# A stream of attention maxima shifted by 75 of a group's 144 events, and unread products in TensorE's waits

## The reference

```python
h = _layernorm(x) * (1 + ca) + sa
q, k, v = split(h @ W_qkv.T + b_qkv)                  # 16 heads of 16, 2 x 2048 tokens
logits = einsum('bhqd,bhkd->bhqk', q, k) / sqrt(16);  causal mask
attn = softmax(logits);  o = einsum('bhqk,bhkd->bhqd', attn, v)
x = x + ga * (o @ W_out.T + b_out)
h = _layernorm(x) * (1 + cb) + sb
x = x + gb * mole(relu(mole(h, W1, ...)), W2, ...)    # base product + softmax-routed low-rank experts
```

## Time and profile before

| | |
|---|---|
| median of three runs | 1465.85 us (1465.51 to 1467.76) |
| profiled execution | span 1465.0 us from its first to its last instruction; the page gives no other time of it |
| TensorE busy | 1309.6 us, 89% |
| VectorE busy | 1022.1 us, 70% |
| ScalarE busy | 773.8 us, 53% |
| GpSimd busy | 172.6 us, 12% |
| mean granted TensorE clock | 0.921 of full |
| attention | 134 to 1119 us: first group's maxima alone from 142 to 232 us, eight groups from 232 to 1113 us |
| last stage | 1119 to 1465 us |

### The profile page before, as it was taken

How to read it: one execution, slowest core, us unless ns; L and a number is a source line. 1 busy time by engine, 2 the same in 40 slices (tenths; PEclk the granted TensorE clock), 3 DMA queues, 4 the chain that set the end, 5 groups by cost and what they waited for, 6 DMA issues and landing times. The chain is left out here.

```text
span 1465.0 us, 25799 instructions
## 1 busy us (share of the span) xinstructions
PE 1309.6 (89%) x8432; PEld 679.2 (46%) x8432; DVE 1022.1 (70%) x1862; ACT 773.8 (53%) x1009; POOL 172.6 (12%) x101
## 2 busy tenths in 40 slices
PE   4993899999999998999998999999994599999997
PEld 3872223333333333333433433433221588888886
DVE  4893997886886885886887688688300466666664
ACT  2771004665665664666565666566793244444443
POOL 1468100000000000000000000000001122222221
PEclk8996557999999999999999999999997699999999
DMA  6345400002102101200210300200003102222200
GB/s 204 123 165 165 131 1 11 21 16 58 33 18 50 40 17 35 56 19 15 65 26 4 74 18 16 63 6 5 10 8 91 44 1 58 58 57 57 57 14 29
DMA packets 75812, 71.07 MB, mean 49 GB/s; under 512 B 17816, under 2 KB 68704, under 8 KB 75688
## 3 DMA queue, kind: packets, MB, share of 16 engines
q1 hardware_dynamic: 75688, 69.51, 16.9%
HBM read 47.57 MB, written 21.23 MB: 47 GB/s over the span
## 5 line engine op out<-in xcount | busy, mean ns | idle before, releaser
L854 DVE TENSOR_REDUCE mx<-ps 128x1 f32<-128x512 f32 (+3 forms) x1120 | 692.2, 669 | 170.8 <-PE ps L726 105.8
L808 ACT ACTIVATE prob<-ps 128x1024 f32<-128x1024 f32 (+3 forms) x640 | 546.7, 895 | 413.8 <-PE ps L751 260.0
L723 PE MATMUL ps<-kst,qst 96*128 96x512 bf16 (+3 forms) x1280 | 426.4, 374 | 28.4 <-DMA kst<-qk_parts 24.3
L747 PE MATMUL ps<-qst,kst 99*128 99x512 bf16 (+3 forms) x1280 | 362.2, 355 | 11.2 <-issue 7.5
L763 PE MATMUL ps<-prob,vw 128*32 128x512 f32 (+3 forms) x2560 | 303.8, 547 | 0.2
L723 PEld LDWEIGHTS ps<-kst,qst 96*128 96x128 bf16 x1280 | 120.7, 99 | 334.7 <-DVE mx L854 244.9
L747 PEld LDWEIGHTS ps<-qst,kst 99*128 99x128 bf16 x1280 | 118.9, 99 | 147.5 <-ACT prob L808 51.1
L751 PE MATMUL ps<-mask_k,ident_bf 128*128 128x128 bf16 x512 | 106.2, 227 | 0.0
L726 PE MATMUL ps<-mask_q,ident_bf 128*128 128x128 bf16 x512 | 106.0, 232 | 0.0
L926 POOL COPY vw<-v_nat 128x1024 f32 (+1 forms) x8 | 8.3, 1044 | 766.3 <-PE ps L763 766.3
L763 PEld LDWEIGHTS ps<-prob,vw 128*32 128x32 f32 x2560 | 51.0, 109 | 102.0 <-issue 79.6
(11 more groups left out here) (144 smaller groups left out, 1429.5 us busy)
## 6 DMA issues: line engine op xcount, KB each, us to landing
qk_parts<-parts SPq DMA_DIRECT2D x32, 384.0 KB, 2.9
qst<-qk_parts SPq DMA_DIRECT2D x192, 64.0 KB, 2.6
kst<-qk_parts SPq DMA_DIRECT2D x192, 64.0 KB, 2.5
xs<-in_x SPq DMA_DIRECT2D x16, 512.0 KB, 6.3
o_rows<-o_sb SPq DMA_DIRECT2D x128, 32.0 KB, 1.7
o_raw<-o_rows SPq DMA_DIRECT2D x16, 256.0 KB
rd<-rden_rows SPq DMA_DIRECT2D x16, 256.0 KB
out<-y SPq DMA_DIRECT2D x8, 512.0 KB, 3.2
```

The source lines that it names most:

```text
L723: last = pe.matmul(at, q[0:QK_ROWS, J, h0 + h, i % 4 * P:(i % 4 + 1) * P], k[0:QK_ROWS, cb, h0 + h, 0:width], start=True, stop=not diagonal)
L747: last = pe.matmul(ps[:, h, 0:width], kst[c][0:ST_ROWS, t // 4, h, t % 4 * P:(t % 4 + 1) * P], qst[c][0:ST_ROWS, J, h, skip:BLK], start=Tr ...
L808: act.activation(prob[:, n % P_BUFS, 2 * pair:2 * pair + 2, 0:width], ps[:, 2 * pair:2 * pair + 2, 0:width], ACT.Exp).then_inc(exp_done, 1)
L854: dve.tensor_reduce(mx[:, h0:h0 + nh, i % 4, cb], ps[:, bank, 0:nh * width].rearrange("p (h x) -> p h x", h=nh), AX, ALU.max).then_inc(max ...
```

## The change

The stream of events is shifted. `AHEAD` = 69: a group's first 69 events ride in the group before it, in tiles 21 to 39, and its last 75 (the rest of block 2 and block 3, with their turns) in the group itself, in tiles 0 to 20. Block 2's turn (event 86) then comes at tile 4.7 and block 3's (event 143) at tile 20.7, ahead of the tiles 12 and 24 that need them; those of blocks 0 and 1 come at tiles 24.7 and 32.7 of the group before. Ahead of the first group 69 events are made alone instead of 144, and the last group carries 75 instead of none. Every tile has 3.6 events, from its first place on. In SyncE's order the rows of the maxima of blocks 2 and 3 are now written within the group, those of 0 and 1 late in the group before; k and the last q block of the group after next are loaded last; the reciprocals are stored after all of these. VectorE's program is the same but that `invert` comes at product 35.

Beside it TensorE makes products that nobody reads (`UNREAD`): 24 (bf16, 512 columns) after the last sums of attention, and 58, 40 and 12 (fp32r, 512 columns) ahead of `project_out(0)`, `turn(0)` and `route_in(0)`. They wait for nothing and release nothing.

```diff
@@ -90,22 +74,29 @@
 EV = max_events()
 NEV = len(EV)
 assert NEV % S_BUFS == 0
-FIRST_SLOT = 7
 SLOTS_OF_TILE = 3
 
 
+
+AHEAD = 69
+TURN_EVENT = [EV.index(("turn", J)) for J in range(NJ)]
+NEAR_UNITS = [J for J in range(NJ) if TURN_EVENT[J] < AHEAD]
+OWN_UNITS = [J for J in range(NJ) if TURN_EVENT[J] >= AHEAD]
+INVERT_AT = NMU // 4
+
+
 def event_slots():
 
-    slots, done = [], 0
-    for u in range(SLOTS_OF_TILE * NKT):
-        want = min(NEV, max(0, (u - FIRST_SLOT) * NEV // (SLOTS_OF_TILE * NKT - FIRST_SLOT - 2)))
-        slots.append(range(done, want))
-        done = want
-    slots[-1] = range(slots[-1].start, NEV)
-    return slots
+    count = SLOTS_OF_TILE * NKT
+    return [range(u * NEV // count, (u + 1) * NEV // count) for u in range(count)]
 
 
 SLOTS = event_slots()
+
+
+
+
+UNREAD = (24, 58, 40, 12)
 
 
 def alone(eng):
@@ -665,44 +656,59 @@
 
 
 
-            def sync_step(sp, s, c, hs, cur, nxt, far):
-                nhs = hs + c
-                nc_ = 1 - c
-                for J in range(NJ):
-                    if nxt:
-                        sp.wait_ge(max_red, (s + 1) * NEV + EV.index(("turn", J)) + 1)
-                        for a in range(NPART):
-                            sp.dma_start(qst[nc_][QK_ROWS + a:QK_ROWS + a + 1, J],
-                                         mT[a * 16:(a + 1) * 16, J, :]).then_inc(m_in[nc_][J], 16)
-                    if cur and far and J < NJ - 1:
-
+            def load_maxima(sp, s, c, J):
+
+                sp.wait_ge(max_red, s * NEV + TURN_EVENT[J] + 1)
+                for a in range(NPART):
+                    sp.dma_start(qst[c][QK_ROWS + a:QK_ROWS + a + 1, J],
+                                 mT[a * 16:(a + 1) * 16, J, :]).then_inc(m_in[c][J], 16)
+
+            def store_out(sp, s, c, hs, J):
+
+                sp.wait_ge(o_out, s * NJ + J + 1)
+                cols = slice(c * S + J * BLK, c * S + (J + 1) * BLK)
+                for h in range(GH):
+                    sp.dma_start(o_rows[bass.ds(hs * GH + h, 1), :, cols]
+                                 .rearrange("o r t -> (o r) t"),
+                                 o_sb[2 * HD * h:2 * HD * h + HD, J % 2, :]
+                                 ).then_inc(o_stored[J % 2], 16)
+
+                    sp.dma_start(den[32 * J + 8 * h:32 * J + 8 * h + 8, c, :],
+                                 o_sb[2 * HD * h + HD:2 * HD * h + HD + 1, J % 2, :]
+                                 ).then_inc(den_in[J % 2], 16)
+
+            def sync_step(sp, s, c, hs, nxt, far):
+
+                def queries(J):
+                    if far:
                         sp.wait_ge(st_done, s * 2 * NKT + 2 * (1 + max(n for n in range(NKT) if KT[n][0] == J)))
                         load_q(sp, c, hs + 1, J)
-                    if cur and far and J == NJ - 1:
-
-                        sp.wait_ge(st_done, (s + 1) * 2 * NKT)
-                        for j in range(NJ):
-                            load_k(sp, c, hs + 1, j)
-                        load_q(sp, c, hs + 1, J)
-                    if cur:
-                        sp.wait_ge(o_out, s * NJ + J + 1)
-                        cols = slice(c * S + J * BLK, c * S + (J + 1) * BLK)
-                        for h in range(GH):
-                            sp.dma_start(o_rows[bass.ds(hs * GH + h, 1), :, cols]
-                                         .rearrange("o r t -> (o r) t"),
-                                         o_sb[2 * HD * h:2 * HD * h + HD, J % 2, :]
-                                         ).then_inc(o_stored[J % 2], 16)
-
-                            sp.dma_start(den[32 * J + 8 * h:32 * J + 8 * h + 8, c, :],
-                                         o_sb[2 * HD * h + HD:2 * HD * h + HD + 1, J % 2, :]
-                                         ).then_inc(den_in[J % 2], 16)
-                    if cur and J == 1 and not (isinstance(s, int) and s == 0):
-                        store_rden(sp, s - 1, 1 - c, hs - 1 + c)
+
+                load_maxima(sp, s, c, OWN_UNITS[0])
+                for J in NEAR_UNITS:
+                    queries(J)
+                    store_out(sp, s, c, hs, J)
+                for J in OWN_UNITS[1:]:
+                    load_maxima(sp, s, c, J)
+                for J in OWN_UNITS[:-1]:
+                    queries(J)
+                    if nxt:
+                        load_maxima(sp, s + 1, 1 - c, NEAR_UNITS[0])
+                    store_out(sp, s, c, hs, J)
+                for J in NEAR_UNITS[1:]:
+                    if nxt:
+                        load_maxima(sp, s + 1, 1 - c, J)
+                if not (isinstance(s, int) and s == 0):
+                    store_rden(sp, s - 1, 1 - c, hs - 1 + c)
+                if far:
+                    sp.wait_ge(st_done, (s + 1) * 2 * NKT)
+                    for j in range(NJ):
+                        load_k(sp, c, hs + 1, j)
+                    load_q(sp, c, hs + 1, NJ - 1)
+                store_out(sp, s, c, hs, NJ - 1)
 
             def tensor_step(pe, s, c, hs, cur, nxt):
-                g, q, k = s + 1, qst[1 - c], kst[1 - c]
-
-                def event(e):
+                def event(g, gc, gh, e):
                     kind, w = EV[e]
                     bank = S_BANK + e % S_BUFS
 
@@ -716,12 +722,12 @@
                         return
                     J, i, h0, nh, cb, width, diagonal = MU[w]
                     if w == 0 or MU[w - 1][0] != J:
-                        pe.wait_ge(q_in[1 - c][J], loads(hs + c, Q_DMAS))
-                        pe.wait_ge(k_in[1 - c][J], loads(hs + c, K_DMAS))
+                        pe.wait_ge(q_in[gc][J], loads(gh, Q_DMAS))
+                        pe.wait_ge(k_in[gc][J], loads(gh, K_DMAS))
                     for h in range(nh):
                         at = ps[:, bank, h * width:(h + 1) * width]
-                        last = pe.matmul(at, q[0:QK_ROWS, J, h0 + h, i % 4 * P:(i % 4 + 1) * P],
-                                         k[0:QK_ROWS, cb, h0 + h, 0:width], start=True, stop=not diagonal)
+                        last = pe.matmul(at, qst[gc][0:QK_ROWS, J, h0 + h, i % 4 * P:(i % 4 + 1) * P],
+                                         kst[gc][0:QK_ROWS, cb, h0 + h, 0:width], start=True, stop=not diagonal)
                         if diagonal:
                             last = pe.matmul(at[:, width - P:width], ident_bf[:], mask_q[:],
                                              start=False, stop=True)
@@ -729,7 +735,10 @@
 
                 def maxima(slot):
                     for e in SLOTS[slot]:
-                        event(e)
+                        if AHEAD + e < NEV:
+                            event(s, c, hs, AHEAD + e)
+                        elif nxt:
+                            event(s + 1, 1 - c, hs + c, AHEAD + e - NEV)
 
                 def logits(n, pair):
                     J, t = KT[n]
@@ -766,25 +775,24 @@
                     last.then_inc(pv_done, 1)
 
                 if not cur:
-                    for e in range(NEV):
-                        event(e)
+                    for e in range(AHEAD):
+                        event(s + 1, 1 - c, hs + c, e)
                     return
                 for n in range(NKT):
                     logits(n, 0)
-                    if nxt:
-                        maxima(SLOTS_OF_TILE * n)
+                    maxima(SLOTS_OF_TILE * n)
                     if n >= PV_LAG:
                         values(n - PV_LAG, s, c)
                     elif not (isinstance(s, int) and s == 0):
                         values(NKT + n - PV_LAG, s - 1, 1 - c)
-                    if nxt:
-                        maxima(SLOTS_OF_TILE * n + 1)
+                    maxima(SLOTS_OF_TILE * n + 1)
                     logits(n, 1)
-                    if nxt:
-                        maxima(SLOTS_OF_TILE * n + 2)
+                    maxima(SLOTS_OF_TILE * n + 2)
                 if not nxt:
                     for n in range(NKT - PV_LAG, NKT):
                         values(n, s, c)
+                    for _ in range(UNREAD[0]):
+                        pe.matmul(ps[:, 0, :], ident_bf[0:QK_ROWS], kst[c][0:QK_ROWS, 0, 0, :], start=True, stop=True)
 
             def scalar_step(act, s, c, last_step):
                 def copy_out(J, s):
@@ -857,7 +865,7 @@
                         if w in LAST_MU:
                             dve.wait_ge(max_red, g * NEV + e + 1)
                             make_parts(LAST_MU[w])
-                        if w == NMU // 2 and not (isinstance(s, int) and s <= 0):
+                        if w == INVERT_AT and not (isinstance(s, int) and s <= 0):
                             invert(dve, s - 1, 1 - c)
                     assert count[0] == per_s
 
@@ -878,17 +886,18 @@
                 for J in range(NJ):
                     load_q(sp, 0, 0, J)
                     load_k(sp, 0, 0, J)
+                for J in NEAR_UNITS:
+                    load_maxima(sp, 0, 0, J)
                 for J in range(NJ):
```

(21 more changed lines are left out.)

## The result

The changed kernel takes 1410.67 us (median of three, 1410.25 to 1412.92) against 1465.85: ratio 0.962, 95% interval 0.9603 to 0.9637.

What follows compares the result with a forecast made beforehand. VectorE bounds the stretch ahead of the first group, TensorE the middle groups, ScalarE the last group. -46.4 + 17.5 - 3.5 + 3.0 + 0 - 6.1 = -35.5 us, from 1465.85 to 1430.3 us; range 1417 to 1445.

Steps and rivals of the forecast that it cites:

- Step 1: Ahead of the first group: events taken away let the first logits start at 185.68 instead of 232.09 us, -46.4 us.
- Step 2: Last group: 75 events put in, priced by comparing copies with a middle group's, +17.5 us; bounds 13 and 23.
- Step 3: Seven groups keeping 144 events: only spread otherwise, turn's wait among full tiles; -0.5 us each, -3.5 in all, bounds -14 to +7.
- Step 4: VectorE's loop: its way back now falls mid-group at tile 20.7, twice; +3.0 us, bounds 0 to 7.5.
- The ring: Three banks between VectorE and TensorE: would hide 2.4 of 3.74 us of VectorE's way back, leaving 1.4 each.
- Step 5: SyncE's queue: rows of block 2's and 3's maxima land in time, margin 5 us, cost nothing.
- Step 6: Last stage's start: unread products end in time and hold the clock, -6.1 us; bounds 0 and 11.8 us late.
- Rival A: Last stage: clock falls despite unread products, 1436.4 us, or the 58 run at half clock, up to 1448; chance 0.15.
- B: Small tiles: VectorE becomes the pace and its loop is paid in full, +15 us, 1445 us; chance 0.12.
- D: Tile 12, all eight groups: block 2's maxima come late and TensorE stands, slower than before, 1486 us; chance 0.03.
- C: Groups' ends: wait and slow clock there heal, -14 instead of -3.5 us, 1420 us; chance 0.10.

Runs made afterwards that it cites:

- e3_empty_ends: The changed kernel with the old rule of places: same shift, no events in a group's first 2.3 tiles and its last place; 1428.76 us (0.9746).
- e14_ahead69_turn_paired: The changed kernel, 69 events ahead, with the two-event places three earlier, so that block 3's last product and turn share one place; 1419.3 us (0.9676).
- e7_ahead_63: The changed kernel with 63 events ahead instead of 69; 1402.08 us (0.9554).
- e1_no_unread: The changed kernel without any unread products, the shift alone; 1413.57 us (0.963).
- e2_unread_only: The kernel before with the four sets of unread products added and no shift; 1460.52 us (0.9952).
- e8_ahead_60: The changed kernel with 60 events ahead instead of 69; 1426.3 us (0.9723).
- e17_ahead66_filled_turn: The changed kernel with 66 events ahead instead of 69 and seven unread products in TensorE's wait ahead of block 3's turn; 1417.63 us (0.9669).

## Why the prediction was wrong

**Step 1 (events from ahead of the first group) was right**: -46.1 for -46.4 us. The row that gave it was the start of event 69, and the logits take its place to 0.4 us.

**Step 2 (events into the last group) was right, a little high**: +15.2 in the four stretches, where its terms gave 2.7 + 6.4 + 5.6 and the wait of 1.96, 16.7. Block 3 to 0 cost 3.1, 0 to 1 5.6, 1 to 2 6.5 with the wait. With the turn behind its product the same group cost +17.0 (`e3_empty_ends`) and +17.1 (`e14_ahead69_turn_paired`), near the step's 17.5. Its counts of events were off: by the order in the code the copies of blocks 0, 1 and 2 fall in tiles 5, 13 and 25, not 6, 14 and 26, so that 10, 31 and 47 events stood between them before, not 16, 31 and 47, and 15, 29 and 27 in the last group now, not 18, 29 and 24. The comparison of copies with and without events held; VectorE's 0.59 us each, the upper bound, did not come.

**Step 3 (seven groups that keep 144 events) failed.** It said: only spread otherwise, -0.3, with the wait and the clock -0.5 each and -2 at best. Measured are -19.7 us for the seven together with VectorE's loop; without the loop's 1.1 to 1.6 us that is about -21, 3.0 us each, beyond the bound. By first logits and copies, `e3_empty_ends` and `e14_ahead69_turn_paired` split the -19.7 in three:
- *The shift with the old places, -4.1 us* (before to `e3_empty_ends`): steps 3 and 4 together had -3.5 and +3.0, so here the forecast is 3.6 us off.
- *The spread, -7.5 us.* `e3_empty_ends` and `e14_ahead69_turn_paired` both have block 3's turn behind its product, with a wait of 2.0 us, and differ in the places of the events: 1428.76 against 1419.3, 9.5 us, of which the profiles have 2.7 behind attention. The step priced all events alike, 0.2 us where they come and 0.23 where they go. In the kernel after, full tiles of 512 columns without mask take 2.62 us with 3 events and 2.84 with 4, counted from values' start to values' start:

```profile
442.33 1.07 PE L772 MATMUL ps<-prob,vw 128*32 128x512 f32 x8
...
445.17 1.07 PE L772 MATMUL ps<-prob,vw 128*32 128x512 f32 x8
...
447.81 1.07 PE L772 MATMUL ps<-prob,vw 128*32 128x512 f32 x8
```

  One more costs 0.215 us. The same tile without any takes about 2.1 us in the last group, where ScalarE sets the pace; so three cost 0.5, 0.17 each, because the first fill what TensorE would stand idle. The gain is from block 2's to block 3's copy, here of one group in `e3_empty_ends` and in `e14_ahead69_turn_paired`:

```profile
599.79 0.59 ACT L813 COPY o_sb<-ps 128x512 f32<-128x512 f32 x1
...
645.58 0.59 ACT L813 COPY o_sb<-ps 128x512 f32<-128x512 f32 x1
```

```profile
596.76 0.58 ACT L807 COPY o_sb<-ps 128x512 f32<-128x512 f32 x1
...
640.93 0.59 ACT L807 COPY o_sb<-ps 128x512 f32<-128x512 f32 x1
```

  45.8 and 44.2 us. Over the six groups this stretch falls by 9.1 us (283.4 to 274.3), 1.5 us a group, with 57 events instead of 56 in it. Five of the 57 stand in tiles 0 and 1 of the next group, where there were none, so that the tiles of block 3 hold four fewer, 0.9 us at 0.215. Some 0.5 us is block 1's turn, which waits 0.63 us behind its product in `e3_empty_ends` and 0.13 in the other. Blocks 0 to 1 and 1 to 2, with two and four events fewer, fall by 3.7 and 2.5 us, and block 3 to 0 grows by 8.2, with 15 events instead of 10 and block 2's turn with its wait of 0.55 us. So tiles 1 to 5, filled up from what they had, were not free. That tiles 0 and 1 took their five events for next to nothing is read from these sums; no run filled them alone.
- *The turn's place, -8.1 us*, from `e14_ahead69_turn_paired` to after (8.6 between the medians), and 1.9 more in the last group. Before, the turn stood right behind the product that it waits for. In the kernel after, tile 20's logits stand between: 1.42 for 1.96 us, and the clock doesn't fall behind it. The forecast had the fallen clock at the loop's way back and took the wait to move as it was; what the order of places puts between product and turn can be read in the code, and was not. How often the clock falls behind the longer wait changes from kernel to kernel (6 of 8 times in `e14_ahead69_turn_paired`, 3 of 8 in `e3_empty_ends`), so the border between this part and the spread is not sharp.

With the old places and the turn behind its product the shift gives 1428.76: the forecast of 1430.3 is about the price of that kernel. The nearness is in part luck: its seven groups were 3.6 us below the forecast's -3.5 + 3.0, and the stretch behind attention 1.5 above its -6.1.

**Step 4 (VectorE's loop) was right in kind, smaller in size**: the way back shows, 2.1 us of further idle time, twice. The two stretches in which it falls take 35.35 and 35.22 us against 34.48 to 34.74, so 1.1 to 1.6 us in all instead of 3.0. What was sized wrong is the way back, 2.1 us where TensorE's 3.74 was taken as the bound. The ring hid no more than the 2.4 us assumed: of the 2.1 us, 0.5 to 0.9 still reached the end. The Trainium skill's rule on the fetch behind a taken branch (Runtime: NRT & Kernel Launch, Instruction fetch mechanics) agrees with these rows for VectorE too.

**Step 5 (SyncE's order) was right**: no wait for block 2's or 3's rows in the kernel after. The margins of 5 us were near: by the trace of after, block 2's rows land 5.6 us or more ahead of tile 12's logits (431.2 and 437.2 us in one group), block 3's 3.6 to 4.7 ahead of tile 24's (467.1 and 471.1). With 63 ahead the second is used up (463.3 and 463.4 in `e7_ahead_63`), and with 60 TensorE waits 1.2 us on average.

**Step 6 (unread products) was half right.** The 58 ran at 0.23 us each (13.43 us for 58), ended as computed, and nothing waited for them; with them the clock stood at 1.00 from 1066 to 1083 us. The Trainium skill says that activity releases the throttle (TensorE: Matmul & The Clock Gate, Part 1), and these rows agree. But they ended 1.92 us ahead of `project_out(0)`, the clock fell 0.2 us behind that pause, and it took 4.60 us, the price of before. Of -6.1 came -2.6 in this profile, -2.9 in the medians (`e1_no_unread`) and -5.3 in the kernel before (`e2_unread_only`), of which the profile has 1.2 in that stretch; where the others came from was not followed. Rival A was true in part: the clock did fall all the same, but behind the pause ahead of `project_out(0)`; behind the one at the engines' meeting, 1.59 us, it held in this profile and fell in those of `e3_empty_ends`, `e8_ahead_60` and `e17_ahead66_filled_turn`. The 24 products were no use.

**The rivals.** B and D did not come: VectorE has slack, and the rows are in time. C named the place (wait and slow clock at the groups' ends) and the sign, and was capped at -14 because it left out the spread and what the turn's place does to the wait; its 1420 is still 9 us above the result.

## What to carry to other kernels

Price a small piece of work by the tile it goes into: in the kernel after one more costs 0.21 us in a tile that is full, and less in one that has slack, so the spread over the tiles is a term of its own and not rounding. Sum over all stretches, though: here one lost 8.2 us of the 15.4 that the others gained. Ask first why a place was empty: here k was on its way, and spreading alone made the kernel 2.3% slower, while a shift that moved k's first use set it free. For a wait of one engine on another, read in the code what stands between the producer and the waiter; something put there shortens the wait and can keep the clock up.
